# Differential attention with routed experts: score products on 64 rows in both halves of the array, three terms, two steps in a burst

## Chip, cores and metric

The kernel runs on one core of a Trainium2 chip. The metric is the time on the device in microseconds, lower is better.

## What is computed

X has 8 batches of 512 tokens with 256 features. It is normalised to xn, and out = X + attention(xn) + experts(xn). What matters here is the attention, for each of 16 heads:

```
Q, K = xn @ Wq + bq, xn @ Wk + bk      # 512 x 128; Q1, Q2 and K1, K2 are the halves of 64
V = xn @ Wv + bv                       # 512 x 64
A1, A2 = Q1 @ K1.T / 8, Q2 @ K2.T / 8  # 512 x 512 each
P = softmax(A1) - lam * softmax(A2)
O = P @ V
Y = concat of O over heads @ Wo + bo, then a layer norm with gamma, beta, times 0.2
```

The experts are a two-layer network with GELU for the expert (of eight) with the highest probability of each token.

## The kernel before

**Stages.** `front_stage` does the normalisation, the routing and the whole attention up to O. `ffn_and_output_stage` does the experts, Wo and the output, and isn't touched.

**Tiling.** Heads go in pairs: 8 pairs in each of 8 batches, 64 pairs (`NPAIRS`). A pair has 8 steps (`TPP`), numbered `g` over all pairs and `st` = 0 to 7 in a pair. A step is one head `u` and one tile of 128 queries, against all 512 keys, for both maps (A1 and A2, index `m`).

**Precision.** Values in f32 are split into a high part (rounded to fp32r) and a low part (the rest), and a product is the sum of high x high, high x low, low x high. ACT writes the high part (`high_part`, line 548), DVE the low part (`low_part`, 898). P @ V and the transposes take plain f32.

**Stacking.** The contraction of a score is over 64 rows only. In before, `spread_by` (297) sends 16 DMAs a pair on SP's queue, which put the high and the low part of Q in rows 0 to 63 and 64 to 127 of `qs`, and either part of K in both halves of `ks`. `scores` (1102) then takes four products of 128 rows and 512 columns a step: for each map (Q high; Q low) against (K high; K high) and against (K low; K low), so all four terms.

**A step, engine by engine.** PE: `scores(g)` into `p_score[g % 2]`, both maps in banks of their own. DVE: the row maximum of both (961). ACT: two exponentials with row sums (614). DVE: `reciprocals` (926). POOL: map 2 times its factor (480). DVE: `combine` (930) makes `pm`. PE: `transposes` (1116), four of 128x128 into the single bank `p_tr`. ACT: `copy_pT` (560) takes that bank out. When a pair's 8 steps are through, PE multiplies by V in `times_v` (1126): four key tiles, each a product for head 0 in columns 0 to 63 of the array and one for head 1 in columns 64 to 127.

**Waits that set the order.** `scores(g)` waits for both exponentials of `g - 2`. `transposes(g)` waits for `combine(g)` and for `copy_pT(g - 1)`. Each engine works its own instructions off in the order written. Beside these PE projects the next pair: q0, k0, q1, k1 (`project`, 1047, six products of 512 columns each) and V (`values`, 1078).

**Order of PE in before** (loop at 1174): each step has `scores(g)`, then `transposes(g - 4)` (`LAG` = 4), then one thing more: a projection at even `st`, `values` at 3, key tiles 0 and 1 of the pair before at 5, key tiles 2 and 3 of the pair before that at 1, nothing at 7. ACT and DVE go step by step too (599, 956), with `copy_pT(g - 4)` ahead of the exponentials of `g`, and `reciprocals` and `combine` two steps behind the maximum.

## Time and profile before

| | us |
|---|---|
| median of 3 runs | 1817.96 (1817.93 to 1819.9) |
| the profiled execution, its own time | 1818.79 |
| its span | 1817.0 |
| PE busy | 1782.6 (98%) |
| DVE busy | 1544.9 (85%) |
| ACT busy | 1415.0 (78%) |
| POOL busy | 638.4 (35%) |
| mean busy share of the 16 DMA engines, slices 6 to 30 | 0.8 |
| granted clock of TensorE, mean | 0.996 of full |

Score products begin at 24.5 us, the attention's last product on PE at 1462.6 us, the experts at 1463.7 us. How to read the rows: a timeline gives start and length of each instruction or of a merged run of like ones. Instructions of an engine are pipelined, so that the next may start before the length of the one before is over; what an operation costs its engine is the distance from start to start (its pitch), and when its result can be used is start plus length.

### The profile page before, as it was taken

The numbers are of one execution on the slowest core, as the hardware profiler recorded it, in microseconds if no ns is written. First come the engines' busy times: TensorE is split into PE (matmuls) and PEld (weight loads), VectorE is DVE, ScalarE is ACT, GpSimd is POOL, SyncE is SP. The second block draws the span as 40 slices with busy tenths as digits, with TensorE's granted clock in tenths as the row PEclk, the third lists the DMA queues.
The fourth block names the chain that finished last, engine by engine and source line by source line (L and its number), as shares of the span: only waits on it lengthen the run. The fifth ranks groups of instructions, "written<-read, shape, count | busy, mean of one in ns | idle before, by whom it ended". The sixth has DMA issues, their size and how long they took to land. (4 is left out here: it accounts for less than half of the span.)

```text
span 1817.0 us, 32461 instructions
## 1 busy us (share of the span) xinstructions
PE 1782.6 (98%) x10494; PEld 1389.1 (76%) x10494; DVE 1544.9 (85%) x2636; ACT 1415.0 (78%) x3364; POOL 638.4 (35%) x711
## 2 busy tenths in 40 slices
PE   6999999999999999999999999999999999999998
PEld 5777777777777777777777777777767789999998
DVE  4988988899889888988898889888999866887677
ACT  5988888888888888888888888888888776676632
POOL 2443222222222222222222322222226555553265
PEclk8999999999999999999999999999999999999999
DMA  8989988888888888888888888888887667667797
GB/s 248 238 247 258 246 226 218 222 235 220 218 225 239 220 220 229 239 221 218 231 231 223 219 231 235 221 218 224 224 209 198 192 246 261 236 241 249 273 370 301
DMA packets 196277, 427.79 MB, mean 235 GB/s; under 512 B 27824, under 2 KB 91312, under 8 KB 188048
## 3 DMA queue, kind: packets, MB, share of 16 engines
q1 hardware_dynamic: 191264, 411.72, 80.6%
q0 software_dynamic: 4688, 13.51, 2.2%
q8 instruction: 84, 1.38, 0.3%
q10 hardware_dynamic: 160, 0.52, 0.1%
q14 instruction: 81, 0.66, 0.1%
HBM read 175.17 MB, written 49.15 MB: 123 GB/s over the span
## 5 line engine op out<-in xcount | busy, mean ns | idle before, releaser
L614 ACT ACTIVATE e<-p_score,nmax 128x512 f32<-128x512 f32 x1024 | 697.1, 688 | 139.0 <-DVE nmax L961 137.6
L961 DVE TENSOR_REDUCE nmax<-p_score 128x2 f32<-128x1024 f32 x512 | 622.9, 1217 | 150.6 <-PE p_score L1111 146.6
L480 POOL TENSOR_SCALAR e<-e,rrec,lam 128x512 f32<-128x512 f32 x512 | 394.1, 770 | 978.7 <-DVE rrec L928 978.2
L1111 PE MATMUL p_score<-ks,qs 128*128 128x512 f32 x2048 | 581.3, 406 | 7.8 <-DMA ks<-k_parts 5.0
L1111 PEld LDWEIGHTS p_score<-ks,qs 128*128 128x128 f32 x2048 | 366.5, 189 | 178.1 <-issue 60.8
L1074 PE MATMUL p_proj<-xh,w 128*128 128x512 f32 x1024 | 384.7, 417 | 5.9 <-DVE k_parts L903 4.5
L935 DVE SCALAR_TENSOR_TENSOR pm<-e,rrec 128x512 f32<-128x512 f32 x512 | 383.3, 749 | 0.4 <-POOL e L480 0.2
L566 ACT COPY pT<-p_tr 128x512 f32<-128x512 f32 x512 | 301.7, 589 | 99.1 <-PE p_tr L1123 98.8
L1123 PEld LDWEIGHTS p_tr<-consts,pm 128*128 128x128 f32 x2048 | 249.6, 140 | 79.9 <-issue 19.8
L1123 PE MATMUL p_tr<-consts,pm 128*128 128x128 f32 x2048 | 308.9, 273 | 1.4 <-ACT pT L566 1.2
L1140 PE MATMUL p_pv<-pT,v 128*64 128x512 f32 x1024 | 247.7, 605 | 0.7 <-ACT pT L566 0.7
L1074 PEld LDWEIGHTS p_proj<-xh,w 128*128 128x128 f32 x1024 | 193.1, 189 | 40.5 <-DVE k_parts L903 5.2
L614 ACT ACTIVATION_READ_ACCUMULATOR e<-p_score,nmax 128x1 f32 x1024 | 205.2, 200 | 0.0
L1074 PE MATMUL p_proj<-xl,w 128*128 128x512 f32 x512 | 200.3, 391 | 0.0
L1140 PEld LDWEIGHTS p_pv<-pT,v 128*64 128x64 f32 x1024 | 62.2, 136 | 95.6 <-issue 94.7
L1854 PE MATMUL p_h<-xsp,w1p 128*128 128x256 f32 (+1 forms) x1104 | 131.6, 277 | 3.6 <-issue 2.2
L1854 PEld LDWEIGHTS p_h<-xsp,w1p 128*128 128x128 f32 x1104 | 128.2, 189 | 5.7 <-issue 5.5
L1572 ACT ACTIVATE h<-p_h,b 128x256 f32<-128x256 f32 (+1 forms) x184 | 70.9, 436 | 69.2 <-PE p_h L1854 68.4
L1875 PE MATMUL p_y<-w2p,hp 128*128 128x256 f32 x936 | 117.1, 284 | 0.0
L1875 PEld LDWEIGHTS p_y<-w2p,hp 128*128 128x128 f32 x936 | 113.5, 191 | 0.0
L1520 POOL TENSOR_TENSOR w2p<-w,w2p 128x2048 fp32r<-128x2048 f32 (+1 forms) x16 | 73.9, 4617 | 97.6 <-ACT w2p L1591 69.6
L1074 PEld LDWEIGHTS p_proj<-xl,w 128*128 128x128 f32 x512 | 97.5, 190 | 12.1
(215 smaller groups left out, 1850.9 us busy)
## 6 DMA issues: line engine op xcount, KB each, us to landing
ks<-k_parts SPq DMA_DIRECT2D x510, 256.0 KB, 4.9
qs<-q_parts SPq DMA_DIRECT2D x512, 128.0 KB, 4.6
w<-weight_parts_scratch SPq DMA_DIRECT2D x56, 1024.0 KB, 10.5
w<-in_w SPq DMA_DIRECT2D x46, 1024.0 KB, 7.2
oT_parts_scratch<-oT SPq DMA_DIRECT2D x32, 512.0 KB, 6.4
op<-oT_parts_scratch SPq DMA_DIRECT2D x16, 1024.0 KB, 9.2
wv<-weight_parts_scratch SPq DMA_DIRECT2D x56, 256.0 KB, 5.5
weight_parts_scratch<-w SPq DMA_DIRECT2D x8, 1024.0 KB, 5.4
```

Source lines behind the costliest of these rows:

```text
L480: nc.gpsimd.tensor_scalar(e2, e2, rrec[:, g % 4, 1:2], lam[:, 0:1], ALU.mult, ALU.mult).then_inc(s_e2, 1)
L566: nc.scalar.copy(pT[pair % 2][st // QT][:, :, qt * P:(qt + 1) * P], p_tr[:, :, :]).then_inc(s_pT, 1)
L614: nc.scalar.activation(ex[:, g % EX, m, :], p_score[g % 2][:, m, :], ACT.Exp, bias=nmax[:, g % 2, m:m + 1], accum_out=rsum[:, g % 4, m:m + ...
L935: vec.scalar_tensor_tensor(out=pm[:, g % 4, :], in0=ex[:, g % EX, 0, :], scalar=rrec[:, g % 4, 0:1], in1=ex[:, g % EX, 1, :], op0=ALU.mult ...
L961: vec.tensor_reduce(nmax[:, g % 2, :], p_score[g % 2][:, :, :], AXX, ALU.max, negate=True).then_inc(s_max, 1)
L1074: last_op = nc.tensor.matmul(bank[:, :], weights(j, a, what[0], u, k), x_part(batch, b, k, 0, S), start=(k == 0 and c == 0), stop=(k == KT ...
L1111: last_op = nc.tensor.matmul(p_score[g % 2][:, m, :], qs[j][u][:, m, qt * P:(qt + 1) * P], ks[j][u][:, m, part, :], start=(part == 0), sto ...
L1123: last_op = nc.tensor.transpose(p_tr[:, k, :], pm[:, g % 4, k * P:(k + 1) * P], ident)
L1140: last_op = nc.tensor.matmul(p_pv[u * D:(u + 1) * D, :], v[it % 2][:, k, c:c + D], pT[j][u][:, k, :], start=(k == 0), stop=(k == QT - 1))
L1520: nc.gpsimd.tensor_tensor(w2p[j][:, 1, 0:f, :], w2[j][:, 0:f, :], w2p[j][:, 0, 0:f, :].bitcast(F32), ALU.subtract).then_inc(s_w2lo, 1)
L1854: last_op = nc.tensor.matmul(p_h[g % 2][:, f % 2, 0:t.fs * P], w1p[j][:, a, k, f * P:(f + 1) * P], xsp[j][:, b, k, 0:t.fs * P], start=(k = ...
L1875: last_op = nc.tensor.matmul(p_y[j][:, s, :], hp[j][:, a, f, s * P:(s + 1) * P], w2p[j][:, b, f, :], start=(f == 0 and c == 0), stop=(f == ...
```

## The change

Four things.

**Scores.** `qs`, `ks`, `spread_by` and the semaphores `s_dup` go, with all 16 DMAs a pair. `scores` reads `q_parts` and `k_parts` directly, which now exist twice (by `pair % 2`). A step has six products of 64 rows and 512 columns: three terms (low x low is left out), for each term map 0 in rows 0 to 63 and map 1 in rows 64 to 127 of the array, in turn. The outputs lie in two banks as before.

**Bursts.** PE's loop advances two steps: `scores(g)`, `scores(g + 1)`, `transposes(g - 2)`, projections or `values`, `transposes(g - 1)`, `times_v`. q0 and k0 both come at `st` 0, `values` at 2, q1 at 4, k1 at 6.

**Runs with V.** They belong to the pair before and stand last in an iteration, so directly ahead of the next score burst: key tile 0 at `st` 2, key tile 1 at 4, key tiles 2 and 3 at 6.

**ACT and DVE** follow in iterations of two steps, as the diff shows. `beside` holds what DVE did beside the steps before: normalising, moments, routing; `split_weights` what ACT did for the weights' high parts in the first pairs.

```diff
-        parts = {"q": [sb(f"q_parts{u}", [P, 2, S], F32R) for u in range(2)],
-                 "k": [sb(f"k_parts{u}", [P, 2, S], F32R) for u in range(2)]}
-        qs = [[sb(f"qs{j}{u}", [P, 2, S], F32R) for u in range(2)] for j in range(2)]
-        ks = [[sb(f"ks{j}{u}", [P, 2, 2, S], F32R) for u in range(2)] for j in range(2)]
+        parts = [{x: [sb(f"{x}_parts{j}{u}", [P, 2, S], F32R) for u in range(2)] for x in "qk"} for j in range(2)]
...
-        AT_STEP = {0: "q0", 2: "k0", 4: "q1", 6: "k1"}
-        V_STEP = 3
-        PV_FIRST, PV_LAST = 5, 1
-        FIND_AT = (0, 2, 3, 4)
+        TERMS = ((0, 0), (0, 1), (1, 0))
+        PROJECTED = {0: ("q0", "k0"), 4: ("q1",), 6: ("k1",)}
+        FIRST_HALF = {0: "q0", 4: "q1", 6: "k1"}
+        SECOND_HALF = {2: "k0"}
+        V_STEP = 2
+        PV_AT = {2: (0,), 4: (1,), 6: (2, 3)}
+        FIND_AT = {0: (0,), 2: (1, 2), 4: (3,)}
...
-        def spread_by(queue, u, what, pair, maps=range(2)):
...
@@ ACT @@
-                if pair >= 1:
-                    act.wait_ge(s_dup[1 - j][u], 16 * DUPS * ((pair - 1) // 2 + 1))
+                if pair >= 2:
+                    act.wait_ge(s_score, TPP * (pair - 2) + QT * (u + 1))
...
+            for g in range(0, STEPS, BURST):
+                pair, st = g // TPP, g % TPP
+                if g >= 2 * BURST:
+                    copy_pT(g - BURST - 1)
+                if st in SECOND_HALF and pair + 1 < NPAIRS:
+                    high_part(pair + 1, SECOND_HALF[st])
+                if st == BURST and group_at(pair):
+                    x_high(group_at(pair))
+                if st == 0 and pair >= 2:
+                    copy_o(pair - 2)
+                exponentials(g)
+                if g >= BURST:
+                    copy_pT(g - BURST)
+                if st in FIRST_HALF and pair + 1 < NPAIRS:
+                    high_part(pair + 1, FIRST_HALF[st])
+                exponentials(g + 1)
...
+                split_weights(pair, st)
+                split_weights(pair, st + 1)
...
@@ DVE @@
+            for g in range(0, STEPS, BURST):
+                pair, st = g // TPP, g % TPP
+                maximum(g)
+                maximum(g + 1)
+                if g >= BURST:
+                    combine(g - 1)
+                if st in SECOND_HALF and pair + 1 < NPAIRS:
+                    low_part(pair + 1, SECOND_HALF[st])
+                if st == BURST and group_at(pair):
+                    x_low(group_at(pair))
+                if st == 0 and pair >= 2 and not whole(pair - 2):
+                    low_o(pair - 2)
+                reciprocals(g)
+                if st in FIRST_HALF and pair + 1 < NPAIRS:
+                    low_part(pair + 1, FIRST_HALF[st])
...
+                if st == V_STEP and pair + 1 < NPAIRS:
+                    add_bv(pair + 1)
+                beside(g)
+                combine(g)
+                reciprocals(g + 1)
+                beside(g + 1)
...
@@ PE @@
+                q, k = (parts[pair % 2][x][u] for x in "qk")
                 if qt == 0:
-                    pe.wait_ge(s_dup[j][u], 16 * DUPS * (pair // 2 + 1))
+                    pe.wait_ge(s_lo, 4 * pair + 2 * u + 2)
                 if g >= 2:
                     pe.wait_ge(s_exp, 2 * g - 2)
-                for m in range(2):
-                    for part in range(2):
-                        last_op = nc.tensor.matmul(p_score[g % 2][:, m, :],
-                                                   qs[j][u][:, m, qt * P:(qt + 1) * P], ks[j][u][:, m, part, :],
-                                                   start=(part == 0), stop=(part == 1))
+                for i, (a, b) in enumerate(TERMS):
+                    for m in range(2):
+                        rows = slice(m * D, (m + 1) * D)
+                        last_op = nc.tensor.matmul(p_score[g % 2][:, m, :], q[rows, a, qt * P:(qt + 1) * P],
+                                                   k[rows, b, :], start=(i == 0), stop=(i == 2))
...
-            for g in range(STEPS):
+            for g in range(0, STEPS, BURST):
                 pair, st = g // TPP, g % TPP
                 scores(g)
-                if g >= LAG:
-                    transposes(g - LAG)
-                if st == PV_FIRST and 1 <= pair < NPAIRS - 1:
-                    times_v(pair - 1, (0, 1))
-                if st == PV_LAST and pair >= 2:
-                    times_v(pair - 2, (2, 3))
...
+                scores(g + 1)
+                if g >= BURST:
+                    transposes(g - BURST)
+                if st == 0 and group_at(pair):
+                    transpose_x(group_at(pair))
...
+                for what in PROJECTED.get(st, ()):
+                    if pair + 1 < NPAIRS:
+                        project(pair + 1, what)
...
                 if st == V_STEP and pair + 1 < NPAIRS:
                     values(pair + 1)
...
+                if g >= BURST:
+                    transposes(g - 1)
+                if pair >= 1 and st in PV_AT:
+                    times_v(pair - 1, PV_AT[st])
```

## Rows read from the trace of the kernel before

**Rows 1.** The page of before: its span, the engines' busy time, the clock by slices.

```profile
span 1817.0 us, 32461 instructions
...
PE 1782.6 (98%) x10494; PEld 1389.1 (76%) x10494; DVE 1544.9 (85%) x2636; ACT 1415.0 (78%) x3364; POOL 638.4 (35%) x711
...
PEclk8999999999999999999999999999999999999999
```

**Rows 2.** The chip's timeline, PE alone: start us, us, engine, line, op, tiles, shape, count.

```profile
916.51 1.18 PE L1111 MATMUL p_score<-ks,qs 128*128 128x512 f32 x4
...
919.38 1.10 PE L1111 MATMUL p_score<-ks,qs 128*128 128x512 f32 x4
920.31 0.60 PE L1123 MATMUL p_tr<-consts,pm 128*128 128x128 f32 x4
920.84 1.94 PE L1140 MATMUL p_pv<-pT,v 128*64 128x512 f32 x8
922.71 1.20 PE L1111 MATMUL p_score<-ks,qs 128*128 128x512 f32 x4
923.74 0.60 PE L1123 MATMUL p_tr<-consts,pm 128*128 128x128 f32 x4
924.10 0.47 PE L1074 MATMUL p_proj<-xh,w 128*128 128x512 f32 x1
...
925.57 1.09 PE L1111 MATMUL p_score<-ks,qs 128*128 128x512 f32 x4
...
926.85 0.49 PE L1097 MATMUL p_proj<-wv,xh 128*128 128x264 f32 x2
...
928.39 1.08 PE L1111 MATMUL p_score<-ks,qs 128*128 128x512 f32 x4
...
938.61 0.71 PE L1111 MATMUL p_score<-ks,qs 128*128 128x512 f32 x2
```

**Rows 3.** The timeline of PE's weight loads (PEld) around one run with V.

```profile
910.98 0.14 PEld L1140 LDWEIGHTS p_pv<-pT,v 128*64 128x64 f32 x2 [0.29 <-issue]
911.41 0.14 PEld L1140 LDWEIGHTS p_pv<-pT,v 128*64 128x64 f32 x2 [0.28 <-issue]
```

**Rows 4.** The timeline of all engines inside the last pair, no projections beside it.

```profile
1443.49 1.23 DVE L961 TENSOR_REDUCE nmax<-p_score 128x2 f32<-128x1024 f32 x1 [1.19 <-PE p_score L1111]
...
1444.75 0.69 ACT L614 ACTIVATE e<-p_score,nmax 128x512 f32<-128x512 f32 x1 [0.24 <-DVE nmax L961]
...
1447.09 0.59 ACT L566 COPY pT<-p_tr 128x512 f32<-128x512 f32 x1 [0.89 <-PE p_tr L1123]
...
1447.82 0.63 PE L1123 MATMUL p_tr<-consts,pm 128*128 128x128 f32 x4
```

**Rows 5.** The timeline of ACT inside the pair of rows 2.

```profile
917.62 0.69 ACT L614 ACTIVATE e<-p_score,nmax 128x512 f32<-128x512 f32 x1 [0.23 <-DVE nmax L961]
...
918.96 0.58 ACT L566 COPY pT<-p_tr 128x512 f32<-128x512 f32 x1
```

**Rows 6.** The page, costliest groups: busy us, mean ns of one | idle before, releaser.

```profile
L614 ACT ACTIVATE e<-p_score,nmax 128x512 f32<-128x512 f32 x1024 | 697.1, 688 | 139.0 <-DVE nmax L961 137.6
L961 DVE TENSOR_REDUCE nmax<-p_score 128x2 f32<-128x1024 f32 x512 | 622.9, 1217 | 150.6 <-PE p_score L1111 146.6
```

**Rows 7.** The timeline of DVE where a tile of V with logits is added.

```profile
907.41 1.22 DVE L961 TENSOR_REDUCE nmax<-p_score 128x2 f32<-128x1024 f32 x1 [0.20 <-PE p_score L1111]
908.55 0.74 DVE L935 SCALAR_TENSOR_TENSOR pm<-e,rrec 128x512 f32<-128x512 f32 x1
909.21 0.16 DVE L922 TENSOR_TENSOR lg<-p_proj,swb 128x8 f32<-128x8 f32 x1
...
910.02 0.15 DVE L928 RECIPROCAL rrec<-rsum 128x2 f32<-128x2 f32 x1
```

**Rows 8.** Who waited for whom at the start: us in total, times, longest.

```profile
PEld p_score L1111 <- DMA ks<-k_parts: 6.2, 2, 5.2
```

**Rows 9.** Busy times of the last pair: us, PE PEld DVE ACT POOL busy, clock.

```profile
1428.95:1463.70 34.75, 31.25 (x192) 20.91 (x190) 26.78 (x40) 27.29 (x59) 13.04 (x17) 1.00 0.54 173
```

More of the change, by code:

```diff
@@ L201, in front_stage @@
         s_w, s_wv = [sem(f"a_w{j}") for j in range(2)], [sem(f"a_wv{a}") for a in range(2)]
-        s_dup = [[sem(f"a_dup{j}{u}") for u in range(2)] for j in range(2)]
         s_xhi, s_xlo = sem("a_xhi"), sem("a_xlo")
@@ L295, in front_stage @@
         HALF = KT * 2 * P
-        def spread_by(queue, u, what, pair, maps=range(2)):
-            j = pair % 2
-            src = parts[what][u]
-            for m in maps:
-                a = src[m * D:(m + 1) * D]
-                if what == "q":
-                    for part in range(2):
-                        queue.dma_start(qs[j][u][part * D:(part + 1) * D, m, :].bitcast(F32),
-                                        a[:, part, :].bitcast(F32)).then_inc(s_dup[j][u], 16)
-                else:
-                    for half in range(2):
-                        queue.dma_start(ks[j][u][half * D:(half + 1) * D, m, :, :].bitcast(F32),
-                                        a[:, :, :].bitcast(F32)).then_inc(s_dup[j][u], 16)
         block = ctx.enter_context(nc.Block())
@@ L358, in load_wv @@
                                  ).then_inc(s_wv[a], 16)
-            def spread(u, what, pair):
-                n = 4 * pair + 2 * u + (what == "k")
-                sp.wait_ge(s_lo, n + 1)
-                spread_by(sp, u, what, pair)
             def store_o(pair):
@@ L391, in _ @@
             load_raw(2)
-            for what in "qk":
-                spread(1, what, 0)
             sp.wait_ge(s_wvhi, 2)
@@ L406, in _ @@
                     sp.dma_start(marks[:, :], ins["marks"]).then_inc(s_marks, 16)
-                if pair + 1 < NPAIRS:
-                    for what in "qk":
-                        spread(0, what, pair + 1)
                 if pair >= 2:
@@ L556, in high_part @@
                 b = bias[:, pair % PAIRS, bias_of[what[0]] + u:bias_of[what[0]] + u + 1]
-                nc.scalar.activation(parts[what[0]][u][:, 0, :], bank_of(pair, what)[:, :],
+                nc.scalar.activation(parts[j][what[0]][u][:, 0, :], bank_of(pair, what)[:, :],
                                      ACT.Identity, bias=b).then_inc(s_hi, 1)
@@ L597, in _, with exponentials @@
             high_qk(1, 1)
-            for g in range(STEPS):
-                pair, st = g // TPP, g % TPP
-                if st == 2 and pair >= 2:
-                    copy_o(pair - 2)
-                what = AT_STEP.get(st - 1)
-                if what and pair + 1 < NPAIRS:
-                    high_part(pair + 1, what)
-                if st == X_STEP + 1 and group_at(pair):
-                    x_high(group_at(pair))
-                if g >= LAG:
-                    copy_pT(g - LAG)
+            def exponentials(g):
                 for m in range(2):
@@ L616, in _, with split_weights @@
                                          accum_out=rsum[:, g % 4, m:m + 1]).then_inc(s_exp, 1)
-                if g == EXP_STEP:
-                    act.wait_ge(s_rd, SHIFTED)
-                    nc.scalar.activation(exr[:, :, :], lg[:, :, :], ACT.Exp).then_inc(s_re, 1)
-                if g == 3:
+            def split_weights(pair, st):
+                if pair == 0 and st == 3:
                     high_v(2)
@@ L642, in _ @@
             next(first)
-            copy_pT(STEPS - 3)
             next(first)
@@ L955, in _, with maximum @@
             route_on = routing()
-            for g in range(STEPS):
-                pair, st = g // TPP, g % TPP
-                if g >= 2:
-                    reciprocals(g - 2)
+            def maximum(g):
                 dve.wait_ge(s_score, g + 1)
@@ L997, in _ @@
                     next(route_on)
+            for g in range(0, STEPS, BURST):
+                pair, st = g // TPP, g % TPP
+                maximum(g)
[11 more added lines that the diff above has]
+                    low_part(pair + 1, FIRST_HALF[st])
+                if g == 0:
+                    dve.wait_ge(s_bv, 32)
+                    add_bv(0)
+                if st == V_STEP and pair + 1 < NPAIRS:
[4 more added lines that the diff above has]
+                beside(g + 1)
             assert next(route_on, "over") == "over"
-            for g in range(STEPS - 2, STEPS):
-                reciprocals(g)
-            combine(STEPS - 2)
             combine(STEPS - 1)
@@ L1192, in _ @@
                     values(pair + 1)
-                if st == X_STEP and group_at(pair):
-                    transpose_x(group_at(pair))
-            transposes(STEPS - 4)
-            times_v(NPAIRS - 2, (0, 1))
-            transposes(STEPS - 3)
-            times_v(NPAIRS - 2, (2, 3))
+                if g >= BURST:
+                    transposes(g - 1)
+                if pair >= 1 and st in PV_AT:
+                    times_v(pair - 1, PV_AT[st])
             transposes(STEPS - 2)
```

61 lines of the change are left out of this document (19 added, 42 removed).

## Prediction, made before the changed kernel was run

> **What bounds the kernel now.** I read the page first. PE is busy 98% of the span at full clock, DVE 85%, ACT 78% [rows 1]: the kernel looks bound by PE. That says little of the waits after an edit that reorders PE's work, so next comes PE's timeline over one pair. A pair takes 938.61 - 916.51 = 22.10 us [rows 2], and there are 64. The blocks lie end to end: four score products take 920.31 - 919.38 = 0.93 us (0.23 each), four transposes 0.36, a projection 925.57 - 924.10 = 1.47, `values` 1.54. From the transposes to a run with V pass 0.53 us, which is 0.36 and 0.17 for the change of the array's mode; the run itself takes 1.87, and the score block behind it 1.03 instead of 0.93 [rows 2]. So a pair is 8 x (0.93 + 0.36) + 4 x 1.47 + 1.54 + 2 x (1.87 + 0.17 + 0.10) = 22.0: PE hardly waits. It can, because its transposes run four steps behind its scores. The waits of ACT for DVE and of DVE for PE [rows 6] cost nothing.
>
> The third view is the last pair. It has no projections, so PE is short of work there and the latencies lie open [rows 4]: from the start of a maximum to its exponentials 1444.75 - 1443.49 = 1.26 us, and from the end of `copy_pT` (1447.09 + 0.59 = 1447.68) to the first transpose 0.14. From ACT's row, the two exponentials hold ACT for 918.96 - 917.62 = 1.34 [rows 5]. These make the new chain.
>
> **The change: PE's work.** Gone is one product of 0.23 per step *if* two 64-row products run beside each other in both halves: three pairs of 0.23 for four products of 0.23, so 8 x 0.23 = 1.84 us a pair. No 64-row product stands in the trace. The nearest rows are the runs with V, whose two products lie side by side in column halves: their weight loads come by twos at 910.98 and 911.41, so a pair of products passes each 0.43 us [rows 3], and four such pairs (1.72) fill the run of eight [rows 2]. Side by side works in columns; I take it to work in rows, at 0.23 a pair. The bounds are 0.23 (full) and 0.46 (one after the other).
>
> Added are changes of mode. Now a pair has four (into and out of two runs). After, four bursts are entered and left and three runs with V entered: 11. At 0.17 each the 7 more cost 1.19 us. PE's work per pair then is 22.10 - 1.84 + 1.19 = 21.45 us. The change of mode to 64 rows isn't in the trace; it may cost nothing or twice 0.17.
>
> The Trainium skill (TensorEngine Tiling (Array Packing), Key Properties) speaks against the change here: switching the tiling mode drains the engine. The trace agrees, with 0.17 us into the runs with V [rows 2]; without that rule PE's work would be 20.26 us.
>
> **The change: the order.** This decides. I follow one iteration from U, the start of `maximum(g)` on DVE. The exponentials of g start at U + 1.26 and hold ACT for 1.34; only then stands `copy_pT(g - 2)`, 0.59. `transposes(g - 1)` waits for it, since `p_tr` is one bank, and starts 0.14 later, at U + 3.33. Behind it on PE, in program order, lie `times_v` and the next score burst, whose first block releases the next maximum. So the iteration is a ring:
>
> - maximum to exponentials 1.26, exponentials 1.34, copy 0.59, to the transpose 0.14, to the run with V 0.53: 3.86
> - the run: 1.87 with two key tiles (`st` 6); with one (`st` 2 and 4) two pairs less, 1.87 - 0.86 = 1.01
> - `scores(g + 2)` until its maximum starts: the block behind a run lasts 1.20 for four products [rows 2], so 1.20 - 0.23 + 0.03 = 1.00
>
> That gives 5.87 us for `st` 2 and for 4, and 6.73 for 6. When does PE arrive at that transpose without waiting? The burst begins 1.00 ahead of U and lasts 6 x 0.23 + 0.10 = 1.48, the change of mode 0.17, `transposes(g - 2)` 0.36, a projection 1.47: U + 2.48, against U + 3.33. So PE stands still for some 0.85 us in three of four iterations. At `st` 0 two projections (2.94) make PE itself late: 0.48 + 0.17 + 0.36 + 2.94 + 0.36 + 0.17 + 1.00 = 5.48.
>
> Do ACT and DVE bind before? Both exponential pairs (the second to its sums, 1.34 and 0.1), the copy and a high part must pass in turn, then the reciprocal: 1.26 + 1.34 + 0.5 + 0.57 + 1.45 + 0.15 = 5.3 us, where 0.5 and 0.57 are estimates, the lengths less the 0.1 by which ACT's instructions overlap [rows 5]. They don't, but they put a floor of 5.3 under any iteration.
>
> A pair: 5.48 + 5.87 + 5.87 + 6.73 = 23.95, against 22.10: 1.85 us more. For 63 pairs +117 us.
>
> **Smaller terms.** In 15 pairs with logits the run with V at `st` 2 waits for `add_bv`. DVE gets there behind two maxima (pitch 1.14), a combine (0.66), the low part of k0 (0.66) and a reciprocal (0.15), at 3.75, and needs 910.02 - 909.21 = 0.81 [rows 7], so V is there at 4.64, some 0.85 late: +13. In 14 pairs that take in x of the next batch, the run waits for `x_low` (another 0.6 on DVE): 0.57 x 14 = +8. Moments of the next batches run beside on DVE, partly past its slack: +6. The first scores no longer wait 5.2 us for the copies' DMA [rows 8]: -5. The 16 DMAs a pair cost nothing now, as no score block in the middle waits for them, so their going gives nothing there. On SP's queue `store_o`, `load_wv`, `load_raw`, `store_w` and `load_w` stood between spreads and behind their waits for low parts; they now go out earlier, each still behind its own wait, and nobody waited for them. The new wait of `high_part` (for scores two pairs back) and of `scores` (for the low part of k) are long met. The low x low term's absence is the product already counted; the second set of `q_parts` and `k_parts` only removes a wait. The last pair takes 34.75 us now [rows 9], as everything drains four steps late. After: 4.86 + 5.87 + 5.87 for three iterations and about 12.5 for the last with its tail, 29: -5.
>
> **Sum.** The profiled execution has its own time of 1818.8 (span 1817.0 [rows 1] and 1.8 around it), 0.8 above the median. 1818.8 + 117 + 13 + 8 + 6 - 5 - 5 = 1952.8; on the median's scale 1952 us. If changes of mode at 64 rows cost nothing, `st` 0 falls to its floor and the others by 0.10: 23.5, so 1925. If they cost twice, five more in the ring: +0.85 a pair, so 2006.
>
> **Rivals.**
>
> *Faster: PE's work rules.* The ring doesn't close, PE finds its transposes ready, and a pair takes the 21.45 us of PE's work. 64 x -0.65 = -42, less 10 for start and end: 1767; 1691 if changes of mode are free. It needs `copy_pT(g - 2)` out by U + 2.48, 0.85 earlier than my sum. For it: PE is the busiest engine. Against it: the copy stands behind both exponentials of g in ACT's own order, and those have their measured lengths.
>
> *Half hidden weights.* Two halves side by side, but the next weights of a half load only when its product is through. A weight load and a 128-column product share 0.09 us in the transposes, so a pair costs 0.23 + 0.09, a step 0.27 more, in the ring once per iteration and once more at `st` 0: 5 x 0.27 = 1.35 us a pair, +86: 2038. Against it: 128-row products with new weights each pass at 0.23 today [rows 2], so their loads are hidden.
>
> The Trainium skill (TensorE: Matmul & The Clock Gate, Part 3) has this as its rule: weight loads overlap running products only where the row groups differ. The trace doesn't bear it out for 128 rows.
>
> *The change doesn't do what it says.* The 64-row products run one after the other: a step takes 1.38 instead of 0.69. 5 x 0.69 = 3.45 us a pair, +221: 2173. Only the column halves speak against it.
>
> **Chances.** Forecast 0.72, faster 0.08, near no change (a ring shorter in several terms) 0.02, half hidden 0.08, one after the other 0.10. The forecast alone holds 1915 to 2010; reaching to the half-hidden case on one side, and leaving out the two far cases, the range is 1890 to 2045. A measurement can tell 0.2% (3.6 us) from no change: faster 0.08, same 0.02, slower 0.90.
>
> **What would show it.** Right: PE busy below 95% in the attention, with transposes that wait for the copy `pT` some 0.8 us in three of four iterations; iterations of about 5.5, 5.9, 5.9, 6.7 us in PE's timeline; score starts of the two halves nearly together and three such pairs in 0.7 us; DVE and ACT each with more idle time; DMA share well below 0.8. Wrong: a copy that starts ahead of the exponentials' end or transposes that never wait (then 1767); or six score products at even distances of 0.23 (then 2173). The weakest point is the price of the 64-row products and their changes of mode; next, that latencies read in the last pair hold in the middle.

## The result and the profile after

After: 1949.69 us, the median of 4 runs (1947.34 to 1951.11), beside 1818.07 (1817.93 to 1819.9) for before. The ratio is 1.072, with a 95% interval of 1.0702 to 1.0739: 7.2% slower, 131.6 us. Forecast were 1952 us, range 1890 to 2045, slower with a chance of 0.90. The profiled execution took 1949.57, span 1947.7, at a granted clock of 0.997 (before 0.996).

The page of after: busy times, DMA by slices, the queue of SP, and costly groups: one of ACT, one of DVE, one of PE (busy us, mean ns of one | idle before, releaser).

```profile
PE 1773.8 (91%) x11518; PEld 1265.0 (65%) x11518; DVE 1558.9 (80%) x2636; ACT 1386.8 (71%) x3364; POOL 640.7 (33%) x711
...
DMA  6233222222222222222222222222211148666797
...
q1 hardware_dynamic: 109504, 210.85, 31.3%
...
L568 ACT ACTIVATE e<-p_score,nmax 128x512 f32<-128x512 f32 x1024 | 699.7, 696 | 384.4 <-DVE nmax L934 384.4
...
L934 DVE TENSOR_REDUCE nmax<-p_score 128x2 f32<-128x1024 f32 x512 | 602.2, 1218 | 143.4 <-PE p_score L1099 142.9
L1110 PE MATMUL p_tr<-consts,pm 128*128 128x128 f32 x2048 | 326.6, 282 | 132.3 <-ACT pT L532 131.8
```

Against [rows 1], PE falls from 98% busy to 91%, and it now waits 131.8 us in all for the copies `pT`. The exponentials wait 384.4 us for the maxima instead of 137.6 [rows 6]. ACT, DVE and PE all have slack: nothing is saturated. The DMA engines' share falls from 0.8 to 0.2 in the attention, and neither the maxima nor the exponentials became shorter by it (a maximum from 1217 to 1218 ns, an exponential from 688 to 696).

PE over one pair, from the burst of `st` 0 to the next; then ACT and DVE at its `st` 6.

```profile
655.95 1.65 PE L1099 MATMUL p_score<-k_parts,q_parts 64*128 64x512 f32 x12
657.53 0.66 PE L1110 MATMUL p_tr<-consts,pm 128*128 128x128 f32 x4
657.95 0.47 PE L1060 MATMUL p_proj<-xh,w 128*128 128x512 f32 x1
...
660.78 0.60 PE L1110 MATMUL p_tr<-consts,pm 128*128 128x128 f32 x4
661.31 1.78 PE L1099 MATMUL p_score<-k_parts,q_parts 64*128 64x512 f32 x12
...
665.64 0.63 PE L1110 MATMUL p_tr<-consts,pm 128*128 128x128 f32 x4 [0.54 <-ACT pT L532]
666.20 1.08 PE L1127 MATMUL p_pv<-pT,v 128*64 128x512 f32 x4
667.21 1.66 PE L1099 MATMUL p_score<-k_parts,q_parts 64*128 64x512 f32 x12
...
671.55 0.63 PE L1110 MATMUL p_tr<-consts,pm 128*128 128x128 f32 x4 [0.70 <-ACT pT L532]
...
673.11 1.67 PE L1099 MATMUL p_score<-k_parts,q_parts 64*128 64x512 f32 x12
...
676.37 0.40 PE L1060 MATMUL p_proj<-xh,w 128*128 128x512 f32 x1
677.46 0.63 PE L1110 MATMUL p_tr<-consts,pm 128*128 128x128 f32 x4 [0.70 <-ACT pT L532]
678.02 1.94 PE L1127 MATMUL p_pv<-pT,v 128*64 128x512 f32 x8
679.88 0.50 PE L1099 MATMUL p_score<-k_parts,q_parts 64*128 64x512 f32 x2
```

```profile
675.39 0.69 ACT L568 ACTIVATE e<-p_score,nmax 128x512 f32<-128x512 f32 x1 [1.58 <-DVE nmax L934]
...
676.73 0.58 ACT L532 COPY pT<-p_tr 128x512 f32<-128x512 f32 x1
```

```profile
674.13 2.35 DVE L934 TENSOR_REDUCE nmax<-p_score 128x2 f32<-128x1024 f32 x2 [0.49 <-PE p_score L1099]
```

The pair takes 679.88 - 655.95 = 23.93 us, its iterations 5.36, 5.90, 5.90 and 6.77, where [rows 2] have 22.10. The ring of `st` 6 can be read off, from the start of the maximum, U = 674.13: exponentials at U + 1.26, the copy at U + 2.60, the transposes at U + 3.33, the run with V at U + 3.89, the next burst at U + 5.75. PE's last product before the wait starts at 676.37 and would be followed by the next 0.23 later, at U + 2.47. So PE stands 677.46 - 676.60 = 0.86 us; the 0.70 in the row counts from the product's modelled end.

Where the 130.7 us between the two spans come from, part by part (after against before): first scores at 19.89 against 24.54 us, -4.7; the first 63 pairs 1540.9 against 1404.4, +136.4; from the last pair's first burst to the experts 34.79 against 34.73 [rows 9], +0.1; the rest of the span 352.2 against 353.3, -1.1.

### The profile page after: what moved, and what is told of

Its sections match the earlier page's. It is cut to its first block and busy times, and to the rows that moved or that the text cites. A ratio compares the mean times of both kernels' runs of the same rounds, so it can differ in the third digit from the quotient of the medians.

```text
span 1947.7 us, 33481 instructions
## 1 busy us (share of the span) xinstructions
PE 1773.8 (91%) x11518; PEld 1265.0 (65%) x11518; DVE 1558.9 (80%) x2636; ACT 1386.8 (71%) x3364; POOL 640.7 (33%) x711
## 3 DMA queue, kind: packets, MB, share of 16 engines
q1 hardware_dynamic: 109504, 210.85, 31.3%
## 5 line engine op out<-in xcount | busy, mean ns | idle before, releaser
L568 ACT ACTIVATE e<-p_score,nmax 128x512 f32<-128x512 f32 x1024 | 699.7, 696 | 384.4 <-DVE nmax L934 384.4
L934 DVE TENSOR_REDUCE nmax<-p_score 128x2 f32<-128x1024 f32 x512 | 602.2, 1218 | 143.4 <-PE p_score L1099 142.9
L1110 PE MATMUL p_tr<-consts,pm 128*128 128x128 f32 x2048 | 326.6, 282 | 132.3 <-ACT pT L532 131.8
L1099 PE MATMUL p_score<-k_parts,q_parts 64*128 64x512 f32 x3072 | 431.9, 412 | 1.0 <-ACT e L568 0.9
L1110 PEld LDWEIGHTS p_tr<-consts,pm 128*128 128x128 f32 x2048 | 219.2, 140 | 297.0 <-DVE pm L910 197.9
L1099 PEld LDWEIGHTS p_score<-k_parts,q_parts 64*128 64x128 f32 x3072 | 265.8, 185 | 221.7 <-issue 112.5
L1060 PE MATMUL p_proj<-xh,w 128*128 128x512 f32 x1024 | 366.7, 409 | 3.7 <-issue 2.1
L1127 PE MATMUL p_pv<-pT,v 128*64 128x512 f32 x1024 | 264.1, 615 | 19.1 <-DVE v L898 12.0
L568 ACT ACTIVATION_READ_ACCUMULATOR e<-p_score,nmax 128x1 f32 x1024 | 215.5, 210 | 0.0
L878 DVE SCALAR_TENSOR_TENSOR q_parts<-p_proj,bias,q_parts 128x512 fp32r<-128x512 f32 x128 | 96.1, 751 | 78.5 <-ACT q_parts L523 74.9
L878 DVE SCALAR_TENSOR_TENSOR k_parts<-p_proj,bias,k_parts 128x512 fp32r<-128x512 f32 x128 | 95.6, 747 | 47.1 <-ACT k_parts L523 47.1
```

Of the source, the lines that this page charges most:

```text
L568: nc.scalar.activation(ex[:, g % EX, m, :], p_score[g % 2][:, m, :], ACT.Exp, bias=nmax[:, g % 2, m:m + 1], accum_out=rsum[:, g % 4, m:m + ...
L878: vec.scalar_tensor_tensor(out=parts[j][what[0]][u][:, 1, :], in0=bank_of(pair, what)[:, :], scalar=b, in1=parts[j][what[0]][u][:, 0, :].b ...
L934: vec.tensor_reduce(nmax[:, g % 2, :], p_score[g % 2][:, :, :], AXX, ALU.max, negate=True).then_inc(s_max, 1)
L1060: last_op = nc.tensor.matmul(bank[:, :], weights(j, a, what[0], u, k), x_part(batch, b, k, 0, S), start=(k == 0 and c == 0), stop=(k == KT ...
L1099: last_op = nc.tensor.matmul(p_score[g % 2][:, m, :], q[rows, a, qt * P:(qt + 1) * P], k[rows, b, :], start=(i == 0), stop=(i == 2))
L1110: last_op = nc.tensor.transpose(p_tr[:, k, :], pm[:, g % 4, k * P:(k + 1) * P], ident)
```

## The experiments

The theory under test: the slowdown is the ring alone, `copy_pT(g - 2)` behind both exponentials with the burst behind it. The rivals: the 64-row products or their changes of mode cost the time; ACT or DVE lack time; PE's order matters in another way. "Per pair" means a pair without logits or x, from burst to burst. Ratios are to before, run beside. Kernels with 64-row products leave out low x low, as after does; those with stacked products have all four terms.

### Each half of the change alone

**rows_old_order** has the new scores in the old order; **burst_stacked** has the new order with before's stacking, copies and 128-row products.

```diff
@@ rows_old_order, against before @@
-                for m in range(2):
-                    for part in range(2):
+                for i, (a, b) in enumerate(TERMS):
+                    for m in range(2):
...
@@ burst_stacked, against after @@
-                for i, (a, b) in enumerate(TERMS):
-                    for m in range(2):
+                for m in range(2):
+                    for part in range(2):
```

> The new score products (64 rows, three terms, no copies by DMA) in the step-by-step order of before. Theory (the added time is the ring maximum, exponentials, copy of pT, transpose, run with V, scores, which the burst order closes): there is no such ring here, PE stays full. The changed kernel's trace has a score block at 0.80 us (before 0.93) and 0.16 us from transposes into scores: 8 x -0.13 + 8 x 0.16 = +0.2 us a pair, and 0.05 more behind each transpose block, +0.4. So 22.3 to 22.8 us a pair, 1825 to 1860 us, 1845 most likely. Rival (the 64-row products and their changes of mode are what costs): at least 1900 us, since this order changes mode about twice as often as the changed kernel.

> The burst order of the changed kernel with the stacked 128-row score products and copies by DMA of before. Theory (ring): the ring stays and its score block grows by 0.20 us (1.23 for 1.03) in three of four iterations, the one at st 0 by some 0.06: 24.6 us a pair for 23.95, 1990 us. Rival (64-row products and their changes of mode cost the time): near 1818 to 1860 us, since no 64-row product is left.

Measured: rows_old_order 1837.92 us (1834.75 to 1840.83), ratio 1.0092 [1.0072, 1.0113], 22.51 us per pair, PE 98% busy. burst_stacked 2004.05 (2001.75 to 2005.15), 1.1013 [1.0993, 1.1033], 24.75 per pair. PE in rows_old_order, then in burst_stacked:

```profile
608.76 0.66 PE L1086 MATMUL p_tr<-consts,pm 128*128 128x128 f32 x4
609.34 0.96 PE L1075 MATMUL p_score<-k_parts,q_parts 64*128 64x512 f32 x6
610.24 0.66 PE L1086 MATMUL p_tr<-consts,pm 128*128 128x128 f32 x4
610.65 0.48 PE L1036 MATMUL p_proj<-xh,w 128*128 128x512 f32 x1
...
612.20 0.96 PE L1075 MATMUL p_score<-k_parts,q_parts 64*128 64x512 f32 x6
```

```profile
690.72 0.63 PE L1147 MATMUL p_tr<-consts,pm 128*128 128x128 f32 x4 [0.58 <-ACT pT L568]
```

What follows: the order costs 186 us with stacked scores (1818 to 2004) and 112 with 64-row scores (1838 to 1950); the scores cost 20 in the old order and give 54 in the new. In the old order a block of 64-row products takes 0.90 us, three pairs of 0.23 and about 0.10 each behind the first pair and at the exit, where four stacked products took 0.93 [rows 2], and the transposes behind it 0.41 instead of 0.36: nothing is won, eight times a pair. On top come the entries: from the start of a projection to the block behind it pass 612.20 - 610.65 = 1.55 us instead of 1.47, and behind transposes a block starts 609.34 - 608.76 - 0.41 = 0.17 later. Only behind a run with V is the block itself shorter than before, 0.90 instead of 1.03. Together a pair takes 22.51 us instead of 22.09, and the first 63 pairs take 24.4 us more; the start, without the copies' DMA, gives 5.0 back. In a burst six pairs share one entry and one exit, 1.59 us, where eight stacked products take 1.96 to 1.97. The waits for the copy stand in burst_stacked too: they belong to the order.

### Are the halves side by side because the products alternate?

**maps_apart** issues the three products of map 0 ahead of the three of map 1.

```diff
-                for i, (a, b) in enumerate(TERMS):
-                    for m in range(2):
+                for m in range(2):
+                    for i, (a, b) in enumerate(TERMS):
```

> The changed kernel with the score products of map 0 all before those of map 1, so that neighbours lie in the same half of the array (only the third of map 0 and the first of map 1 can run side by side). Theory (pairs run side by side because neighbours lie in different halves): a block takes 5 products' time for 3, 0.46 us more; in the ring three times and twice at st 0: 2.3 us a pair, 2095 us; if nothing overlaps at all, 0.69 and 2170 us. Rival (the halves work independently, whatever the order): no change, 1950 us.

Measured: 1954.34 us (2 runs, 1953.78 and 1954.9), 1.0738 [1.0713, 1.0763], 23.99 to 24.0 per pair.

```profile
659.04 1.66 PE L1099 MATMUL p_score<-k_parts,q_parts 64*128 64x512 f32 x12
660.63 0.55 PE L1110 MATMUL p_tr<-consts,pm 128*128 128x128 f32 x3
```

My expectation was wrong, its rival right. The burst takes 660.63 - 659.04 = 1.59 us as in after, though three products on the same rows stand in a row. Had they run in program order, a half would have stood idle through most of each block. The trace has the first two products of the burst start within 10 ns of each other (3 to 4 ns in after). Its records don't name the half; I read the two as one of each map: the half that is free takes its own products while those issued ahead wait for theirs. The order in the program is worth 5 us of 1950 here. That the maps alternate isn't what makes the change work.

### Shorten the ring

**copy_between** puts `copy_pT(g - 2)` between the two exponentials of g. **copy_and_combine_early** also puts `combine(g - 1)` between the two maxima.

```diff
@@ ACT, both @@
-                exponentials(g)
+                exponentials(g, (0,))
                 if g >= BURST:
                     copy_pT(g - BURST)
+                exponentials(g, (1,))
@@ DVE, copy_and_combine_early only @@
                 maximum(g)
-                maximum(g + 1)
                 if g >= BURST:
                     combine(g - 1)
+                maximum(g + 1)
```

> The changed kernel with the copy of pT (step g - 2) between the two exponentials of step g instead of behind both; ACT does the same work in all. Theory (ring): the transpose of g - 1 can start 0.67 us earlier, and PE, which waits 0.9 us for it now, gains that: iterations of about 5.36, 5.3, 5.3, 6.1 us, of which the 5.3 are the floor of ACT and DVE; 22.1 us a pair, 1833 us; up to 1850 if the later second exponential delays DVE. Rival (the price of the 64-row products, or DVE, sets the pace): no gain, 1945 to 1960 us.

Measured: 1917.13 us (1916.99 to 1918.49), 1.0536 [1.0517, 1.0555], 23.26 per pair. My expectation was right in sign and 84 us too low. All engines of copy_between at `st` 4:

```profile
654.18 2.36 DVE L935 TENSOR_REDUCE nmax<-p_score 128x2 f32<-128x1024 f32 x2
...
656.12 0.58 ACT L532 COPY pT<-p_tr 128x512 f32<-128x512 f32 x1
...
656.46 0.74 DVE L911 SCALAR_TENSOR_TENSOR pm<-e,rrec 128x512 f32<-128x512 f32 x1
...
657.25 0.55 PE L1111 MATMUL p_tr<-consts,pm 128*128 128x128 f32 x3 [0.45 <-DVE pm L911]
```

The copy is out at 656.70, U + 2.52, as it should. The transposes start at U + 3.07, since `combine(g - 1)` stands behind both maxima on DVE and ends at 657.20. A second ring lay 0.26 us below the first. Taking both away:

> The copy of pT between the two exponentials, as in the run before that, and in addition DVE's combine of g - 1 between the two maxima instead of behind both. In that run the transposes of g - 1 no longer followed the copy but started 0.06 us behind the end of combine, 3.0 us after the maximum of g. Theory (two rings, the second through combine, close behind the first): with both early the transposes can start 2.66 us after the maximum, and the iterations are about 5.37, 5.3, 5.35, 6.13 us: 22.15 us a pair, 1835 us. Rival (ACT and DVE were at their floor already at 5.67 us): stays at 1917 us.

Measured: 1866.9 us (1865.46 to 1869.22), 1.0255 [1.0234, 1.0276]. Per pair 22.15 at best, as expected (up to 22.4 behind a pair with logits). The total was 32 us above the expectation, because of pairs that take x of the next batch or have logits (23.5 to 24.1). One such pair, at `st` 2 (PE of copy_and_combine_early):

```profile
656.04 0.63 PE L1111 MATMUL p_tr<-consts,pm 128*128 128x128 f32 x4
657.80 1.08 PE L1128 MATMUL p_pv<-pT,v 128*64 128x512 f32 x4 [1.13 <-DVE xl L663]
```

The run with V could come earlier now, and `x_low` doesn't: its wait was 0.46 us in after and is 1.13 here.

### Lengthen the ring

**extra_in_ring** adds one copy of 128x512 on ACT (of `bv` to a spare tile) ahead of `copy_pT(g - 2)`; **extra_beside** adds the same one behind the exponentials of g + 1.

```diff
@@ extra_in_ring; extra_beside has the same lines behind exponentials(g + 1) @@
                 exponentials(g)
                 if g >= BURST:
+                    act.wait_ge(s_bv, 32)
+                    nc.scalar.copy(spare[:, :], bv[:, 0:S])
+                if g >= BURST:
                     copy_pT(g - BURST)
```

> The changed kernel with one more ACT instruction per iteration, a copy of 128x512 numbers of the bias rows into a spare tile that nobody reads, between the two exponentials of step g and the copy of pT of g - 2. It should hold ACT for some 0.5 us. Theory (ring): it delays the transpose of g - 1 by its whole length in the iterations at st 2, 4 and 6, and pushes st 0 over its floor by about 0.45: 4 x 0.5 = 2.0 us a pair, 2075 us. If the wait for combine, 0.26 us behind the copy's way in the run with the copy between the exponentials, were the one that came last here too, 0.26 of each would be free; by the changed kernel's trace it comes first, so nothing is. Rival (ACT has idle time, 71% busy, and is not in the chain): no change, 1950 us.

> The same extra ACT instruction once per iteration, but behind both exponentials of step g + 1, in the gap of some 1.4 us in which ACT waits for the next maximum. Theory (ring): off the ring, nearly free, 0 to 0.1 us a pair: 1950 to 1956 us. Rival (ACT's total work counts): the same added time as with the instruction in the ring.

Measured: extra_in_ring 2056.35 us (2054.73 to 2057.71), 1.1296 [1.1273, 1.1319]; extra_beside 1952.43 (1951.02 to 1954.67), 1.0727 [1.0703, 1.0752]. ACT and PE of extra_in_ring:

```profile
713.80 0.61 ACT L599 COPY spare<-bv 128x512 f32<-128x512 f32 x1
...
714.31 0.59 ACT L533 COPY pT<-p_tr 128x512 f32<-128x512 f32 x1
...
715.05 0.63 PE L1114 MATMUL p_tr<-consts,pm 128*128 128x128 f32 x4 [1.22 <-ACT pT L533]
```

The same operation costs 107 us in one place and 3 in the other. Its pitch is 714.31 - 713.80 = 0.51 us, and PE's wait grows from 0.70 to 1.22, by 0.52. This shows the ring, and that ACT's time as such isn't short. A pair grows by 2.0: 0.52 at `st` 4 and at 6, 0.96 at `st` 2, where the second score block now waits for exponentials too, and 0.05 at `st` 0. The expectation had 0.5 in each of the four. Its total was 19 us too high, as pairs with logits or x grew by 1.0 to 1.4 only.

### How much of the order can be won back

Four kernels that keep bursts and 64-row products. **best1**: as copy_between; `combine(g - 1)` between the maxima at `st` 2 and `reciprocals(g - 1)` there at 4, 6 and 0; at `st` 4 and 6 V ahead of the transposes; `x_low` and `add_bv` earlier. **later_transposes**: the transposes of g - 3 and g - 2 instead of g - 2 and g - 1, with the copy of g - 3 between the exponentials of g; `reciprocals(g - 1)` between the maxima; `x_low` and `add_bv` with logits ahead of the combine. **gaps**: this, with `reciprocals(g)` ahead of the low part of k0, `add_bv` without logits at `st` 4, and the copy ahead of both exponentials at `st` 4 and 6. **gaps_q1_later**: this, with q1's high and low parts moved from the middle of `st` 4 to the start of `st` 6.

```diff
@@ later_transposes, PE, against after @@
-                    transposes(g - BURST)
+                    transposes(g - BURST - 1)
...
-                    transposes(g - 1)
+                    transposes(g - BURST)
@@ gaps, ACT and DVE, against later_transposes @@
+                if g >= 2 * BURST and st >= 4:
+                    copy_pT(g - BURST - 1)
                 exponentials(g, (0,))
...
+                reciprocals(g)
+                if st == BURST and pair + 1 < NPAIRS:
                     low_part(pair + 1, SECOND_HALF[st])
@@ gaps_q1_later, against gaps @@
-        FIRST_HALF = {0: "q0", 4: "q1", 6: "k1"}
-        SECOND_HALF = {2: "k0"}
+        FIRST_HALF = {0: "q0", 6: "k1"}
+        SECOND_HALF = {2: "k0", 6: "q1"}
```

> An attempt at the best order with the new score products: the copy between the exponentials; at st 4 and 6 the run with V ahead of the transposes of g - 1, so that it hides their waits; at st 2 combine of g - 1 between the maxima, and the additions to V and the low part of x ahead of the low part of k0; the reciprocals of g - 1 behind the maximum of g, except at st 2. Theory (PE's own work is the bound once the rings are open): iterations of about 5.37, 5.37, 5.13, 6.0 us, 21.9 us a pair, and the 0.9 us of the pairs with logits gone: 1800 us, 1790 to 1815. Rival (ACT and DVE have a floor of 5.3 us that the order can't lower, and more waits show): 1820 to 1840 us.

Measured: 1885.99 us (1883.78 to 1889.01), 1.0368 [1.0342, 1.0394], 22.85 to 22.9 per pair. Missed by 86 us. PE of best1 at `st` 6:

```profile
646.66 0.96 PE L1106 MATMUL p_score<-k_parts,q_parts 64*128 64x512 f32 x6
648.11 0.96 PE L1106 MATMUL p_score<-k_parts,q_parts 64*128 64x512 f32 x6 [0.49 <-ACT e L568]
```

At `st` 6 the second score block starts 1.45 us behind the first instead of 0.80. The chain that I read in the trace: with `add_bv` and the low part of k0 ahead of `reciprocals(g)`, POOL and the combine at `st` 2 come late, then the maximum of `st` 4, then its exponentials. No run moves this one thing alone; gaps moves it together with others.

> A second attempt at a better order with the new score products: transposes one step later (g - 3 and g - 2 in an iteration), so that combine of g - 1 is on nobody's way; the copy of pT (g - 3) between the exponentials of g; the reciprocals of g - 1 behind the maximum of g, so that the maximum doesn't wait for the exponentials of g - 1; x and, with logits, V split ahead of combine at st 2. Runs with V stay last. Theory (both rings open, DVE below its floor, so PE's own work and 0.3 us of waits rule): iterations of about 5.36, 5.2, 5.25, 5.95 us, 21.75 us a pair, and 0.4 more in pairs that take in x: 1790 us, 1780 to 1810. Rival (ACT's and DVE's floor of 5.3 us stays, from other waits): 1815 to 1835 us.

Measured: 1862.46 us (1861.85 to 1864.81), 1.0239 [1.0225, 1.0253], 22.15 to 22.2 per pair, pairs with logits or x 23.2 to 24.3. Missed by 72 us, and above the rival's 1815 to 1835 as well. In a normal pair `st` 4 takes 5.43 us (5.25 expected) and `st` 6 6.12 (5.95), which is 0.4 a pair and some 25 us in all; the other half of the miss lies in the special pairs.

> The run with the later transposes had a second half of PE's burst that waits for exponentials at st 6, DVE full at st 2, and special pairs (x, logits, moments) of 23.2 to 24.3 us. Here the reciprocals of g come ahead of the low part of k0 at st 2; the addition to V (without logits) moves to st 4 and the low part of O behind the reciprocals, both into gaps in which DVE waits for ACT; and at st 4 and 6 the copy of pT stands ahead of both exponentials. Theory (DVE's order at st 2 delays the maximum of st 4, and the copy the transposes): 0.3 us less in normal pairs, 0.7 in special ones, 1862 - 33 = 1830 us. Rival (ACT's way from a maximum through two pairs of exponentials and a high part to the second score block, at least 5.3 us, holds st 4): 0.1 us less, 1850 us.

Measured: 1824.81 us (6 runs, 1823.78 to 1827.76), 1.0032 [1.0019, 1.0044], 21.95 per pair, 5 us below the expectation. `st` 4 falls to 5.00 to 5.02 us, while `st` 6 takes 6.34, its second score block waiting for exponentials.

> The same, and the high and low part of q1 move from the middle of st 4 to the start of st 6, where ACT waits for the maximum anyway. Theory (the way of ACT above holds st 4 at 5.3 us): it opens, st 4 falls to PE's own 5.05 us and the second score block of st 6 no longer waits: 21.6 us a normal pair, 1800 us. If it beats 1818 us, the new score products are worth having in some order. Rival (DVE has no room for two low parts at st 6): as the run without this step.

Measured: **1805.37 us** (1804.29 to 1808.16), 0.9927 [0.991, 0.9944]. This is faster than before by 0.7% and than after by 7.4%, and 5 us above the expectation. Its page and its PE over a pair:

```profile
PE 1748.2 (97%) x11518; PEld 1274.5 (71%) x11518; DVE 1575.5 (87%) x2636; ACT 1381.8 (77%) x3364; POOL 644.9 (36%) x711
```

```profile
601.23 1.67 PE L1110 MATMUL p_score<-k_parts,q_parts 64*128 64x512 f32 x12
...
611.85 1.65 PE L1110 MATMUL p_score<-k_parts,q_parts 64*128 64x512 f32 x12
...
616.86 1.66 PE L1110 MATMUL p_score<-k_parts,q_parts 64*128 64x512 f32 x12
...
622.73 1.65 PE L1110 MATMUL p_score<-k_parts,q_parts 64*128 64x512 f32 x12
```

This pair takes 622.73 - 601.23 = 21.50 us (its iterations 5.39, 5.23, 5.01 and 5.87) and no row of it shows a wait: PE's own work, for which the prediction had 21.45. So from 23.93 to 21.50, all that the changed order cost in a normal pair was waiting.

**gaps_stacked** is the same with before's stacked products and copies.

```diff
-                for i, (a, b) in enumerate(TERMS):
-                    for m in range(2):
+                for m in range(2):
+                    for part in range(2):
```

> The best order so far (1805 us), with the stacked 128-row score products and the copies by DMA of before: what the new score products are worth once the order is right. Theory (PE's own work rules): per iteration a burst of 1.86 us for 1.60, against 0.16 us less for entering it and 0.05 less behind it: 4 x (0.26 - 0.21) = 0.2 us a pair more, and 5 us more at the start for the copies: 1805 + 13 + 5 = 1823 us, 1815 to 1835. If the mode changes of the 64-row products cost more than the traces show, it comes out below 1805 us; if the score products are worth their 0.13 us a step in full and mode changes nothing, 1870 us.

Measured: 1876.67 us (1874.54 to 1881.89), 1.0314 [1.029, 1.0339], 22.46 per pair.

```profile
634.41 2.12 PE L1146 MATMUL p_score<-ks,qs 128*128 128x512 f32 x8
636.38 0.60 PE L1158 MATMUL p_tr<-consts,pm 128*128 128x128 f32 x4
...
639.57 0.60 PE L1158 MATMUL p_tr<-consts,pm 128*128 128x128 f32 x4
639.92 2.10 PE L1146 MATMUL p_score<-ks,qs 128*128 128x512 f32 x8
```

Missed by 54 us. The burst takes 1.97 instead of 1.60. I had set against this a cheaper way from the transposes into the scores, 639.92 - 639.57 = 0.35 instead of 0.53, but only one burst in four comes behind transposes; behind a run with V both forms pay the same. So the iterations are longer by 0.12 (`st` 0), 0.21, 0.32 and 0.32: 22.46 - 21.50 = 0.96 a pair, 60 us over 63 pairs, and 5 more at the start. Scores of 64 rows are worth 71 us in this order (1876.7 to 1805.4), 54 in the changed one, and -20 in the old. And bursts don't pay by themselves: with stacked products this best order is 3.1% slower than before.

## Why the prediction was right

**What bounds.** "PE hardly waits. It can, because its transposes run four steps behind" held: with the distance cut to one and two steps, PE waits for the copy in three iterations of four, while every engine has slack. At `st` 2 the wait is shorter than the 0.85 us forecast, as `values` and the entry of the burst behind transposes keep PE busy longer than the projection that the sum had there: 5.90 us against PE's own 5.23 in gaps_q1_later, 0.67. gaps_q1_later takes the waits away with PE's work as it is.

**The products.** "I take it to work in rows, at 0.23 a pair" was right. A burst is 1.59 to 1.60 us to the transposes, which is 6 x 0.23 = 1.38, 0.10 more from the first pair to the second (0.33 instead of 0.23, as in the score blocks behind a run [rows 2]), and 0.11 at the end. Where the second block has to wait, the 0.10 comes again: the 1.78 at 661.31 instead of 1.65.

**Changes of mode.** "At 0.17 each" was nearly right. Into 64 rows 661.31 - 660.78 - 0.36 = 0.17. Out of them 0.11 at the burst's end, and four transposes at 0.41 instead of 0.36, together 0.16. From the burst's start to the next block 1.48 + 0.17 + 0.36 = 2.01 was taken, 1.60 + 0.41 = 2.01 measured. PE's work of 21.45 came out at 21.50 in gaps_q1_later. Two small errors hide in that: the two projections at `st` 0 together take 0.11 less than the sum had (see the ring), so the seven more changes cost 21.50 - (22.10 - 1.84 - 0.11) = 1.35 us and not 1.19, 0.19 each.

The Trainium skill (TensorEngine Tiling (Array Packing), Key Properties) says that a change of mode drains the engine. The trace agrees, at 0.17 us into the 64-row products and 0.16 out of them.

**The ring.** Every term held. Exponentials at U + 1.26 and the transposes at U + 3.33 are the predicted values to the hundredth; the run with V comes 0.56 later instead of 0.53, and the maximum 674.13 - 673.11 = 1.02 after the burst instead of 1.00. So 5.90, 5.90 and 6.77 instead of 5.87, 5.87 and 6.73, and PE's wait 0.86 instead of 0.85. `st` 0, PE's own work, took 5.36 instead of 5.48: two projections end to end are 660.78 - 657.95 = 2.83 instead of 2.94, as only the first product behind transposes takes 0.32 to the next (675.12 to 675.44 at `st` 6) and the second projection has none. So 23.93 instead of 23.95, with +0.10 and -0.12 in it. The "floor of 5.3 under any iteration" held for this order of ACT alone: `st` 4 takes 5.01 in gaps_q1_later.

**Smaller terms.** The first 63 pairs gave +136.4 where 117 + 13 + 8 + 6 = 144 were taken. Pair by pair the first takes 25.34 us against 26.20, where the sum had +1.85 for it too: -2.7. What explains it is TensorE's clock, which this term left out. In before's first pair it was granted at 0.50 of full (1.2 GHz) in two stretches, with PE busy all through; in after's first pair it was 1.00. The rows: stretch, its length, busy times of PE, PEld, DVE, ACT and POOL, clock, DMA share, GB/s.

```profile
24.54:28.79 4.25, 4.25 (x10) 3.38 (x11) 1.23 (x1) 0.88 (x3) 0.64 (x1) 0.50 1.04 282
42.44:45.85 3.41, 3.41 (x11) 2.77 (x11) 3.41 (x9) 2.73 (x8) 1.19 (x3) 0.50 1.04 239
```

At half the clock these 7.66 us are worth some 3.8 us, an estimate; with both first pairs at full clock the change would have cost about 3 us there, not 1.85. The other 62 lie 1515.5 - 62 x 23.95 = 30.6 above a normal pair now, and 1378.2 - 62 x 22.10 = 8.0 above it before, so the extras grew by 22.6 and not by 27: -4.4. The waits for `add_bv` and `x_low` were sized well: 14 pairs have 6.83 us at `st` 2 for 5.90, +13 (their working in the prediction gives 4.64 - 3.86 = 0.78 each, and 0.85 was written), and 14 others 6.43, +7. So the +6 for the moments was too high, about 2 is left for it. The start gave -4.7 for -5. That the copies' DMAs go gave nothing in the middle, as said.

**The last pair** is the term that failed: "about 12.5 for the last with its tail, 29: -5". It gave +0.1. Its four iterations took 4.89, 8.10, 6.51 and 15.29 us, 34.79 in all, where 4.86, 5.87, 5.87 and 12.5 were taken, 29.1. PE of after there, then two stretches of it:

```profile
1567.73 3.66 PE L1140 MATMUL p_proj<-high_hot,low_hot 128*128 128x39 f32 x32
...
1571.83 1.98 PE L1127 MATMUL p_pv<-pT,v 128*64 128x512 f32 x4
1573.74 2.28 PE L1099 MATMUL p_score<-k_parts,q_parts 64*128 64x512 f32 x12
...
1584.60 0.63 PE L1110 MATMUL p_tr<-consts,pm 128*128 128x128 f32 x4 [2.09 <-ACT pT L532]
1585.16 3.55 PE L1127 MATMUL p_pv<-pT,v 128*64 128x512 f32 x8
```

```profile
1571.68:1575.09 3.41, 3.41 (x12) 1.45 (x12) 0.32 (x2) 0.59 (x1) 0.77 (x1) 0.50 0.97 389
1585.34:1588.75 3.41, 3.41 (x9) 0.61 (x8) 2.45 (x4) 2.84 (x6) 2.05 (x3) 0.50 0.00 0
```

The largest part is again the clock, granted at 0.50 in these two stretches, where before's last pair had 1.00 [rows 9]. The run with four products takes 1.98 instead of 1.08, the burst 2.28 instead of 1.65, the run with eight 3.55 instead of 1.94: 3.1 us together. Ahead of the second fall PE had stood 2.09 us for the copy; ahead of the first it had worked without a gap since 1565.64. Why the clock fell isn't shown. Another 1.3 us is the routing at `st` 2: PE has 32 products of it there, arrives behind them later than the ring would let it go on, and the iteration takes 7.20 at full clock instead of 5.87. The last 1.2 is in the tail, 13.7 at full clock instead of 12.5, a figure that the prediction had not split up. The ring itself held here too: the transposes of `st` 6 start at 1584.60, U + 3.33, so the 2.09 us are no extra. Its own figures gave 34.75 - 29.1 = 5.7, of which 5 was written.

So the sum was 1952.8 for 1949.6: 7.6 less in the pairs, 5.1 more in the last, 0.3 more at the start, 1.1 less in the experts. Errors of both signs, each under 0.5% of the time. That two of them came from the clock, with 3.8 us against before and 3.1 against after, and nearly cancelled in the difference is luck.

**The rivals.** The point on which the faster one turns, the copy out by U + 2.48, was named well, but not all of it: copy_between had it out at U + 2.52 and was still 5.4% above before, with `combine(g - 1)` next, then `x_low` and `add_bv`, then `reciprocals` behind DVE's parts. With those moved too, its time per pair is there, 21.50. The total isn't 1767 but 1805: the 63 pairs of gaps_q1_later take 1397.7 us, 43 above 63 x 21.50. Its first eight pairs hold 16.5 of these (up to 25.2 us each), the last six 10 (one of 27.4, beside the routing, in which PE stands 2.6 us and then has 3.4 us at half the clock), and logits and x the rest. "Half hidden weights" and "one after the other" fell: a pair of products passes in 0.23, where these need 0.32 and 0.46.

## What to carry to other kernels

When an edit reorders in-order engines, write each ring down as a sum of distances from start to start, and compare it with the time at which the bound engine gets there; the totals of busy time say nothing of it. Where one ring is shortened, work out the second and third before a price is put on it: here the first cut gave 33 of the 144 us that all of them gave together. And price a change of two parts in each order in which it could stand: the same score products cost 20 us in one order and saved 54 and 71 in two others.

## What the chip showed that I hadn't expected

- Products on the two row halves run side by side whatever their order in the program: three of one half issued ahead of three of the other take the same time (maps_apart, 1.59 us for 12). The trace of after shows it another way: the product that raises the semaphore of a block is its last in the program, and in 99 of 512 blocks it starts before another of the same block, by up to 26 ns (at 674.372, the other at 674.398). The Trainium skill (TensorE: Matmul & The Clock Gate, Part 3) has matmuls start and end strictly in program order; these starts don't agree with it, and the measurement decides.
- A run of 64-row products costs 0.23 us a pair plus a fixed price, the same for three pairs and for six: 0.17 ahead of it behind transposes, 0.10 after its first pair, 0.11 behind it, 0.05 in the transposes that follow. Behind a projection the entry costs 0.08 where nothing was paid before. That is why one step per block loses against stacked products and two steps win.
- Taking away 200 MB of DMA (411.72 to 210.85 MB on SP's queue) and three quarters of the DMA engines' share left the lengths of the commonest operations within 10 ns: maxima 1217 to 1218, exponentials 688 to 696, combines 749 to 743, copies `pT` 589 to 598. None became clearly shorter, and ACT's high parts of k became longer, 687 to 720.
